# Second attention: dividing the probabilities by their sums on VectorE instead of GpSimd

## What is computed

```python
def _L1_xattn_ref(x, y, wq, bq, wk, bk, wv, bv, wo, bo):
    q = (x @ wq + bq).reshape(B, SQ, N_HEADS, D_HEAD)        # 8 x 512 x 16 x 32
    k = (y @ wk + bk).reshape(B, SKV, N_HEADS, D_HEAD)       # 8 x 120 x 16 x 32
    v = (y @ wv + bv).reshape(B, SKV, N_HEADS, D_HEAD)
    scores = jnp.einsum('bqhd,bkhd->bhqk', q, k) / jnp.sqrt(jnp.asarray(D_HEAD, x.dtype))
    attn = jax.nn.softmax(scores, axis=-1)
    out = jnp.einsum('bhqk,bkhd->bqhd', attn, v).reshape(B, SQ, D_EMBED)
    return out @ wo + bo

x = x + tanh(g_xattn[0]) * L0_xattn(ctx_768, layernorm(x), mask, ...)
x = x + tanh(g_ffn[0])   * L0_ffn(layernorm(x), ...)      # 8 experts, given routing
x = x + tanh(g_xattn[1]) * L1_xattn(layernorm(x), ctx_768, ...)
x = x + tanh(g_ffn[1])   * L1_ffn(layernorm(x), ...)      # 8 experts, top 2
```

## Time and profile before

| | |
|---|---|
| median of 3 runs | 4306.66 us (4304.27 to 4310.42) |
| the profiled execution's own time | 4306.23 us |
| its span | 4304.5 us |
| granted TensorE clock, mean | 0.961 of full speed |
| TensorE busy | 3971.2 us (92% of the span) |
| VectorE busy | 2977.4 us (69%) |
| ScalarE busy | 1978.6 us (46%) |
| GpSimd busy | 1003.8 us (23%) |

### The profile page before, as it was taken

One profiled execution on the slowest core, in us unless ns is written; L12 is line 12 of the kernel. 1 busy time (PEld: TensorE's weight loads), 2 busy tenths in 40 slices (PEclk: granted clock), 3 DMA queues, 4 the chain that ended last, 5 costly groups with the idle time before them and its releaser, 6 DMA issues. The chain is left out here.

```text
span 4304.5 us, 68747 instructions
## 1 busy us (share of the span) xinstructions
PE 3971.2 (92%) x23968; PEld 3205.2 (74%) x23968; DVE 2977.4 (69%) x4625; ACT 1978.6 (46%) x2806; POOL 1003.8 (23%) x1012
## 2 busy tenths in 40 slices
PE   5999999998589999999987998967999999999998
PEld 3665555564379999999983555547999999999998
DVE  3766666666467667667643788757888888877885
ACT  3655555554144444444422544514444444444443
POOL 3211122210011101101103666403222223322221
PEclk9999999999699999999998999968999999999999
DMA  2000000000166666665632122106766666666664
GB/s 91 22 32 30 30 17 24 28 20 20 59 216 205 208 209 205 208 210 198 208 125 72 45 93 79 40 29 209 212 213 208 214 207 214 209 215 209 211 211 125
DMA packets 376608, 578.80 MB, mean 134 GB/s; under 512 B 25960, under 2 KB 186792, under 8 KB 376488
## 3 DMA queue, kind: packets, MB, share of 16 engines
q1 hardware_dynamic: 344024, 503.50, 35.2%
q0 software_dynamic: 26208, 61.68, 5.7%
q10 hardware_dynamic: 6256, 12.06, 0.8%
HBM read 518.31 MB, written 58.86 MB: 134 GB/s over the span
## 5 line engine op out<-in xcount | busy, mean ns | idle before, releaser
L1111 DVE TENSOR_TENSOR e_WL<-e_raw,e_WH 128x2048 fp32r<-128x2048 f32 x418 | 957.1, 2290 | 474.0 <-ACT e_WH L1060 470.3
L1060 ACT ACTIVATE e_WH<-e_raw 128x2048 fp32r<-128x2048 f32 x418 | 798.8, 1911 | 798.1 <-PE bank L1038 570.3
L1022 PE MATMUL bank<-e_xh,e_WH 128*128 128x256 f32 x3968 | 1126.9, 284 | 38.5 <-ACT e_hf L1076 19.0
L1022 PE MATMUL bank<-e_xl,e_WH 128*128 128x256 f32 x3968 | 1126.2, 284 | 0.0
L1022 PE MATMUL bank<-e_xh,e_WL 128*128 128x256 f32 x3968 | 1126.1, 284 | 0.0
L1022 PEld LDWEIGHTS bank<-e_xh,e_WH 128*128 128x128 f32 x3968 | 765.3, 193 | 42.0 <-issue 28.4
L1022 PEld LDWEIGHTS bank<-e_xl,e_WH 128*128 128x128 f32 x3968 | 765.4, 193 | 2.3
L1022 PEld LDWEIGHTS bank<-e_xh,e_WL 128*128 128x128 f32 x3968 | 765.0, 193 | 0.0
L1038 PE MATMUL bank<-e_WH,e_hh 128*128 128x512 f32 x1360 | 534.9, 393 | 0.0
L1038 PE MATMUL bank<-e_WH,e_hl 128*128 128x512 f32 x1360 | 529.7, 389 | 0.0
L1038 PE MATMUL bank<-e_WL,e_hh 128*128 128x512 f32 x1360 | 529.0, 389 | 0.0
(11 more groups left out here) (216 smaller groups left out, 6131.3 us busy)
## 6 DMA issues: line engine op xcount, KB each, us to landing
e_raw<-in_w SPq DMA_DIRECT2D x262, 1024.0 KB, 5.2
e_raw<-in_w SPq DMA_DIRECT2D x312, 512.0 KB
y<-e_Yo ACTq DMA_DIRECT2D x23, 512.0 KB, 2.9
a_X<-in_x SPq DMA_DIRECT2D x32, 256.0 KB, 2.6
a_R<-in_x SPq DMA_DIRECT2D x32, 256.0 KB, 4.0
x<-a_R SPq DMA_DIRECT2D x32, 256.0 KB, 2.0
a_X<-x SPq DMA_DIRECT2D x32, 256.0 KB, 3.4
x<-a_X SPq DMA_DIRECT2D x32, 256.0 KB, 2.0
```

Source lines behind the costliest of these rows:

```text
L1022: mm = nc.tensor.matmul(up[n % RING][:, q * ROWS:q * ROWS + ROWS], w, x[:, c, :], start=(c == 0 and i == 0), stop=(c == DC - 1 and i == 2))
L1060: act.activation(WH[:, p, :], raw[:, s, :], ACT.Copy).then_inc(high_ready.sem, 1)
L1111: dve.tensor_tensor(WL[:, p, :], raw[:, p % 2, :], WH[:, p, :].bitcast(F32), ALU.subtract)\
```

## The change

The multiplication by the reciprocal, `share`, is taken out of GpSimd's queue and put into VectorE's, in `total` right behind the reciprocal, with the same operands and shape. VectorE waits for its own reciprocal (`rinv_done`) and increments `p_ready` itself. GpSimd keeps everything else, in the same order. Nothing is changed on TensorE, ScalarE and SyncE.

```diff
@@ GpSimd
-                def share(u):
-                    pool.wait_ge(rinv_done, u + 1)
-                    wide = Pr[:, u % 3, :, :, :].rearrange("p h g n -> p (h g) n")
-                    pool.tensor_tensor(wide, wide, rinv[:, u % 3, :].unsqueeze(2).to_broadcast([P, HS, CL]), ALU.mult)\
-                        .then_inc(p_ready, 1)
-
...
-                        if softmax(n):
-                            if s >= QT:
-                                residual(n, s - QT)
-                            share(STEPS1 * n + s)
+                        if softmax(n) and s >= QT:
+                            residual(n, s - QT)
@@ VectorE, total(u)
                     dve.wait_ge(sum_done, u + 1)
                     dve.reciprocal(rinv[:, u % 3, :], ssum[:, u % 3, :]).then_inc(rinv_done, 1)
+                    dve.wait_ge(rinv_done, u + 1)
+                    wide = Pr[:, u % 3, :, :, :].rearrange("p h g n -> p (h g) n")
+                    dve.tensor_tensor(wide, wide, rinv[:, u % 3, :].unsqueeze(2).to_broadcast([P, HS, CL]), ALU.mult)\
+                        .then_inc(p_ready, 1)
```

## The result

| | before | changed |
|---|---|---|
| median | 4306.94 us (4304.27 to 4310.42, 4 runs) | 4338.0 us (4332.59 to 4339.98, 4 runs) |
| the profiled execution | 4306.23 us (span 4304.5) | 4339.25 us (span 4337.5) |

The ratio is 1.007, with a 95% interval of 1.0052 to 1.0087: slower by 31 us. The forecast was +22 us (4328.0), with a range from 4307 to 4346.

The account below looks back on a forecast made before the run. In the second attention's fullest bodies neither VectorE nor TensorE was seen to have much room. Body terms 4.6 + 4.8 + 6.8 + 5.8 gave +22 us, 4306.2 + 22 = 4328.2 us; range 4307 to 4346.

Parts of the forecast that it names:

- a step at VectorE's pace grows by 1.2 us: Second attention: each VectorE step gains the division and the wait for the reciprocal, about 1.2 us.
- Body 0: First batch: steps 4 to 6 pay 1.2 us each, steps 0 to 3 pay 1.0 more; +4.6 us.
- 1.0 us more: Body 0, steps 0 to 3: step 2's maximum waits only 0.26 us for scores, so 1.0 us shows.
- Body 7: Last batch: steps 2 to 6 run at VectorE's pace, five times 1.2 us less 0.2; +5.8 us.
- Bodies 2 to 5: Gathering bodies: early steps leave 2.9 us, step 5 gives back 1.1; +1.7 us each taken, 6.8 in all.
- Bodies 1 and 6: Steps 0 to 3 hide the division, steps 4 and 5 pay 1.2 us each; +2.4 each, 4.8 in all.
- delays only step 7's exponential: Bodies 1 and 6: step 6's division holds up nothing but the next exponential, for which TensorE has spare work.
- over a microsecond: Bodies 1 and 6, step 7: TensorE has that much more work of its own than ScalarE before they meet.
- rival C: Gathering bodies: the lock's waits only change place, 7.4 us a body, +45 in all, 4351 us; chance 0.16.
- some 40 us more: Sign in the changed profile: VectorE's busy time in the second attention grows by this much.
- Rival A: Steps 5 and 6 of bodies 2 to 5: interference goes, TensorE's pace hides the rest; say 4308 us; chance 0.16.
- Rival B: Chain to TensorE's transposes shortens, turns start earlier; at most 5.4 us gained, 4300.8 us; chance 0.05.

Follow-up runs that it names:

- experiment 1: The changed kernel with the division put back on GpSimd in bodies 1 and 6 alone; 4323.6 us, ratio 1.0039.
- experiment 6: The changed kernel plus 16 unread matmuls on TensorE in front of its wait for ScalarE in step 6 of bodies 1 and 6; 4340.56 us.
- experiment 10: The kernel of experiment 9 plus 14 unread matmuls in front of TensorE's wait for ScalarE in step 6 of bodies 1 to 6; 4324.06 us.
- experiment 9: The changed kernel, GpSimd's residuals in steps 2, 3, 4 and 7, its bias and residual additions waiting for the previous step's division; 4328.85 us.
- experiment 11: The kernel before, division on GpSimd, residuals behind it in steps 2 and 3, in front in 4 and 7; 4283.59 us.
- experiment 4: The kernel before, with GpSimd's division put in front of the residual addition instead of behind it; 4304.32 us, ratio 0.9988.

## Why the prediction was right, and where it was not

**The mechanism was right where VectorE sets the pace.** The forecast said that a step at VectorE's pace grows by 1.2 us. Steps 4 to 6 of body 0 went from 4.73, 4.68 and 4.67 to 5.92, 5.91 and 5.91 us; the steps 4 and 5 of body 6 from 6.35 and 6.28 to 7.53 and 7.51. The maxima of body 0 show it (the forecast wanted 5.9 from one to the next):

```profile
2365.01 1.16 DVE L1577 TENSOR_REDUCE a_smax<-bank 128x8 f32<-128x960 f32 x1 [0.63 <-PE bank L1411]
...
2370.93 1.15 DVE L1577 TENSOR_REDUCE a_smax<-bank 128x8 f32<-128x960 f32 x1
...
2376.84 1.15 DVE L1577 TENSOR_REDUCE a_smax<-bank 128x8 f32<-128x960 f32 x1
```

**Body 0**, +4.6: measured +5.45. The three steps gave 3.66. The "1.0 us more" for steps 0 to 3 came as +0.70: they sum to 26.63 before and 27.33 now. Step 7 gave another 1.09, which the forecast did not have; the two waits of TensorE that are named under experiment 1 fall into it, and so does the start of the stretch at 0.50.

**Body 7**, +5.8: measured +5.99.

**Bodies 2 to 5**, 6.8: measured 7.2. In body 4 step 4 grew by 1.47 (1.2 was forecast), step 5 fell by 1.40 (1.1), step 6 by 0.67 (0.8): the exchange of a 4.20 us addition for a division of 2.05 and an addition of 0.68 was read rightly, and so was the bias that holds the division of step 0. Its price was not: step 0 grew by 1.25 (0.5 was forecast), step 1 by 0.51 (1.2). The four differ among each other, from +1.2 to +2.9, with clocks from 0.92 to 0.97, so a part of the agreement in the sum is luck.

**Bodies 1 and 6**, 4.8: measured 12.4. This is the term that failed, and it makes 7.6 of the 9 us by which the stage overran. What the forecast said of the waits held. Steps 4 and 5 grew by 1.2 each in body 6, so ScalarE reached L1522 in step 6 by 2.4 us later, and TensorE waited 2.81 us there instead of 0.40: 2.41 us more, the two divisions and no more. The sentence that step 6's division "delays only step 7's exponential" held too, for it starts only when the wait is over. ScalarE's copy (right behind step 6's exponential, which starts at 2761.95) and VectorE's division in step 6 of body 6:

```profile
2762.86 0.67 ACT L1522 ACTIVATE a_gated<-bank,gate 128x512 f32<-128x512 f32 x1
```

```profile
2764.41 1.16 DVE L1592 TENSOR_TENSOR a_Pr<-a_Pr,a_rinv 128x960 f32<-128x960 f32 x1
```

And the spare of "over a microsecond" that TensorE has behind it was there: with the clock kept up in experiment 6, step 7 takes 7.9 and 8.1 us, 0.7 to 1.0 less than before the change. What failed is the step from the delay to its price. The forecast priced a delay by its own length, 2.4 us a body, and the clock behind the longer wait stood at nothing in its sum, without a reason, though the earlier trace rows showed 1.00 in body 6, where this wait is 0.40 us, and 0.97 in body 4, where it is 3.9. Behind the wait TensorE ran at 1.2 GHz for 4.8 us and below full clock for some time more. Experiment 1 shows that the cost lies in these bodies, experiments 6 and 10 that it hangs on the wait: with products in its place the bodies get shorter though there is more to do.

An estimate from these runs of what the 12.4 us are made of: the forecast's 4.8 are in them. Another 4.4 came back when the waits were filled (2.0 and 2.5, experiment 6). A further 1.6 are the lower clock that body 1 inherits from the end of body 0, which the sum, cut at the bodies' borders, had lost. About 0.8 are a lock that nobody had forecast, in steps 5 and 6 of body 1, where GpSimd's bias (from 2429.14) and residual run beside VectorE's normalisation:

```profile
2430.29 1.64 DVE L1612 TENSOR_SCALAR a_N<-a_X,a_mv,a_rstd 128x512 f32<-128x512 f32 x1
```

A free one takes 0.54 us; in experiment 9, where the bias is paced, it does, and step 5 falls from 7.90 to 7.51 us. The last 0.8 us are not accounted for.

**The total.** 4338.0 lies inside the range of 4307 to 4346, and that is partly luck. The upper part of the range stood for a division of up to 1.87 us and for rival C; the free division took 1.16, as forecast, and the holds cost a gathering body little. What filled the range was the clock, which was in none of its terms. VectorE was to be busy for some 40 us more and was for 54.5; the 19.5 us of held divisions more than account for the difference.

**Rival A** (the interference goes, the rest is hidden) fell: the gathering bodies grew. **Rival B** fell: TensorE's wait for the division was 5.4 us and is 5.3. **Rival C** (the locks change place) was half right. They do, 19.5 us of them, most of them on VectorE's divisions of steps 0, 5, 6 and 7. But the gathering bodies grew by 1.8 us each, not 7.4; experiment 9 took all of the holds away and came to 21 us over the kernel before. That remainder is, as far as the runs show, the 1.2 us a step itself and the clock behind TensorE's waits; experiment 10 takes the larger part of the latter away and leaves bodies 2 to 5 between 3.6 and 5.2 us above those of experiment 11, which have the division on GpSimd.

What neither forecast nor rivals had: the costly thing in the kernel before was not GpSimd's division but **the order in which GpSimd adds its residual**. The change moved 1.16 us a step onto the engine that sets the pace of these steps. The hold that it took away came from two instructions standing back to back in two steps of four bodies. Moving the residual alone (experiment 11) removes the hold and adds nothing to VectorE. Not tested is how much of experiment 11's gain is the hold and how much the clock behind TensorE's wait, which went from 0.95 to 0.97 up to 1.00 in these bodies: the kernel before, with its own waits filled, was not run.

## What to carry to other kernels

Before moving an operation from a slow engine to a fast one, look at which queue sets the step, not at which engine is quicker: here the quicker engine had no room, and the slower one finished two steps ahead of its reader. Where two engines hold each other, try first to move the small operations (here a 1.3 us addition) into steps where the other engine has nothing to be held; and when GpSimd's queue is reordered, follow what stands behind, as its gathers took back the gain in experiment 4. When a delay ends in a wait of TensorE, look at the clock behind it as well: behind the waits of 3.20 and 2.81 us here filling them gave back 2.0 and 2.5 us. The loss is not the same each time. Behind waits of 3.8 and 4.2 us in bodies 4 and 5 of the changed kernel the bodies' clocks were 0.97 and 0.92, by which some 2 and 5 us are lost.

## What the runs showed of the hardware

- A hold by GpSimd can be longer than one of its instructions, and can begin before it. In body 4 of the kernel before, VectorE's addition of step 5 starts at 2607.42, 0.62 us *before* the residual at 2608.04, and still lasts until residual and division are both through the earlier trace rows. GpSimd was issuing the gathers (L1336) at that moment, until 2608.02. The division of step 6 shown above starts in the same way, at 2636.04, 0.17 us before its residual, and lasts 2.48 us. That the issuing of the gathers begins the hold is inferred from these times; no run tests it. In step 4 the same addition, which starts while GpSimd does nothing, takes 0.69 us; GpSimd's division then starts 0.16 us behind it and is the longer one, 2.18 us against 1.79 for a free one:

```profile
2601.26 2.18 POOL L1363 TENSOR_TENSOR a_Pr<-a_Pr,a_rinv 128x960 f32<-128x960 f32 x1 [3.44 <-DVE a_rinv L1597]
```

- The maximum and the subtraction, which read PSUM, and the sum, with one SBUF input, were never held in the changed kernel: the 64 maxima last 1124 to 1159 ns, the subtractions 1156 to 1159, the sums 1119 to 1155. The division, with two SBUF inputs, lasts from 1157 to 2495 ns. But two SBUF inputs are not the only mark: the normalisation L1612, with one tensor and two columns of 128x1 as inputs, lasts 536 ns at the least and 1637 and 1625 in the two places beside GpSimd's additions.
- Behind a wait of 2.81 us TensorE's products took 1.88 us instead of 1.06, 1.97 instead of 1.08 and 1.11 instead of 0.66, with a granted clock of 0.50 over 4.8 us.
- One kernel's bodies are not equally long each time: bodies 2 to 4 are the same program in experiment 6 and in the changed kernel, and took 65.6, 68.3 and 66.5 us there against 64.6, 65.3 and 64.9, with clocks of 0.92, 0.90 and 0.95 against 0.95, 0.95 and 0.97. So a difference of 3 us in one body is told by several bodies or by the runs' median, never by one.
